# In the last quarter of a convolution, x comes doubled from DRAM instead of being doubled by VectorE

## The reference

```python
x = x + ffn(conv(x, cond_2048[:, None, :], b), w_router, w_experts)
# conv: depthwise causal convolution of 8 taps over the sequence, per channel, plus b
y = conv_general_dilated(x, w, window_strides=(1,), padding=[(K - 1, 0)], feature_group_count=D) + b
# ffn: each token goes to the one expert with the largest logit
idx = argmax(einsum('bsh,eh->bse', y, w_router))
out = take_along_axis(einsum('bsh,efh->bsef', y, w_experts), idx)
```

## Time and profile before

| | |
|---|---|
| median of three runs | 513.11 us |
| the profiled execution | 512.61 us, its span 510.8 us, mean granted clock 0.997 |
| TensorE busy | 502.5 us, 98% of the span |
| VectorE busy | 287.6 us (56%) |
| ScalarE busy | 150.5 us (29%) |
| GpSimd busy | 133.2 us (26%) |
| moved by DMA | 130.31 MB, mean 255 GB/s |

### The profile page before, as it was taken

How to read it: one execution, slowest core, us unless ns; L and a number is a source line. 1 busy time by engine, 2 the same in 40 slices (tenths; PEclk the granted TensorE clock), 3 DMA queues, 4 the chain that set the end, 5 groups by cost and what they waited for, 6 DMA issues and landing times.

```text
span 510.8 us, 9483 instructions
## 1 busy us (share of the span) xinstructions
PE 502.5 (98%) x2764; PEld 435.5 (85%) x2765; DVE 287.6 (56%) x418; ACT 150.5 (29%) x255; POOL 133.2 (26%) x148
## 2 busy tenths in 40 slices
PE   8999999999999999999999999999999999999995
PEld 8999999998888888888888888888888888888884
DVE  4947373769885233599753422863266343472961
ACT  2444444286101001365620000610043010340710
POOL 0004325063622111323311312203122322122222
PEclk9999999999999999999999999999999999999998
DMA  8977999999779999699998664695649655534445
GB/s 290 411 221 212 398 282 405 348 346 309 264 253 283 341 350 299 184 348 358 327 395 249 175 198 123 202 372 177 185 133 354 221 165 158 169 116 130 145 142 165
DMA packets 59623, 130.31 MB, mean 255 GB/s; under 512 B 12752, under 2 KB 32720, under 8 KB 59600
## 3 DMA queue, kind: packets, MB, share of 16 engines
q1 hardware_dynamic: 41696, 70.12, 44.3%
q0 software_dynamic: 14832, 54.27, 29.6%
q10 hardware_dynamic: 3072, 5.65, 3.5%
HBM read 94.56 MB, written 35.45 MB: 255 GB/s over the span
## 4 chain that ended last, share of the span: by engine, by line
PE 93%; DMA 5%; issue 0%; POOL 0%; DVE 0%; DVEq 0%; ACT 0%; SPq 0%; POOLq 0%
PE ps L858 75%; PE ps L814 18%; DMA y_sorted<-rows,pos_i 3%; DMA xs<-x_t 2%; DMA xs<-x_both 1%; POOL out L937 0%; DVEq L167 0%; DVE xs L516 0%; PE ps L829 0%; SPq L307 0%; ACT rows L438 0%; ACT part L437 0%; PE ps L826 0%; POOLq L978 0%; DVE x_row L702 0%
## 5 line engine op out<-in xcount | busy, mean ns | idle before, releaser
L858 PE MATMUL ps<-w_sb,ys 128*128 128x512 f32 x1680 | 381.6, 389 | 0.4 <-ACT rows L438 0.4
L858 PEld LDWEIGHTS ps<-w_sb,ys 128*128 128x128 f32 x1680 | 315.2, 188 | 66.1 <-ACT rows L438 0.5
L689 DVE STREAM_TRANSPOSE y_cols<-y_blk 128x1024 f32<-128x1024 f32 x36 | 44.8, 1243 | 140.1 <-PE ps L858 131.6
L814 PE MATMUL ps<-mats,xs 128*128 128x128 f32 x1024 | 117.8, 278 | 1.4 <-DMA xs<-x_both 1.1
L814 PEld LDWEIGHTS ps<-mats,xs 128*128 128x128 f32 x1024 | 116.9, 195 | 1.9 <-DVE mats L508 1.4
L451 ACT CAST ys<-y_cols 128x1024 fp32r<-128x1024 f32 x36 | 37.9, 1052 | 269.4 <-DVE y_cols L689 269.4
L680 DVE TENSOR_TENSOR w_sb<-w_raw,w_sb 128x1024 fp32r<-128x1024 f32 x56 | 64.2, 1218 | 3.3 <-ACT w_sb L446 3.3
L937 POOL DMA_INDIRECT out<-x_row,idx x35 | 40.8, 1165 | 80.3 <-DVE x_row L704 76.4
L944 POOL COPY idx<-ids_all 128x1 int32 (+1 forms) x36 | 15.2, 421 | 173.5 <-DMA out<-x_row,idx 118.7
L446 ACT CAST w_sb<-w_raw 128x1024 fp32r<-128x1024 f32 x56 | 56.4, 1050 | 9.5 <-PE ps L858 8.6
L925 POOL DMA_INDIRECT y_sorted<-rows,pos_i x32 | 35.3, 1103 | 78.1 <-PE ps L814 74.9
(11 more groups left out here) (102 smaller groups left out, 47.7 us busy)
## 6 DMA issues: line engine op xcount, KB each, us to landing
w_raw<-experts SPq DMA_DIRECT2D x56, 512.0 KB, 9.5
y_blk<-y_sorted SPq DMA_DIRECT2D x152, 128.0 KB, 3.4
xs<-x_both SPq DMA_DIRECT2D x15, 512.0 KB, 9.8
xs<-x_t SPq DMA_DIRECT2D x28, 256.0 KB, 7.0
xs<-x_t ACTq DMA_DIRECT2D x20, 256.0 KB, 7.5
w_first<-experts SPq DMA_DIRECT2D x8, 512.0 KB, 9.7
ids_all<-y_sorted SPq DMA_DIRECT2D x38, 1.0 KB, 4.5
x_row<-x_rows,idx POOLq DMA_INDIRECT x36, 4.6
```

The costliest lines, as they stand in the source:

```text
L689: V.transpose(y_cols[k][:, :, :].rearrange("p m (t i) -> p t m i", t=4), y_blk[k][:, :, :, :]).then_inc(y_blocks, 1)
L814: mm = nc.tensor.matmul(to, xs[:, n % X_RING, s % PACK, :], mats[:, s, :].rearrange("p (u n) -> p u n", n=SIDE), start=(s == sets[0]), sto ...
L858: return nc.tensor.matmul(out_ps[k][:, f * HALF:(f + 1) * HALF], ys[k][:, a, c, :], w_sb[:, c, b, f * HALF:(f + 1) * HALF], start=(c == 0 ...
```

## The change

In the last quarter too (packs 48 to 63) x comes from `x_both`: transfers of 512 KB over all 128 partitions in place of 256 KB over 64. VectorE makes no copies there, and TensorE waits for the transfer itself. Everything else stays: the queues, the ring, the order of issue.

```diff
-DOUBLED = PACKS
+DOUBLED = [n for n in range(4 * PACKS) if n < PACKS or n >= 3 * PACKS]
+SINGLE = [n for n in range(4 * PACKS) if n not in DOUBLED]
...
-    both = np.ones((DOUBLED, 2, PHASES, CH, PACK, GROUP, STEPS), x.dtype)
-    for n in range(DOUBLED):
-        both[n, 1 - n % 2] = cur[n]
-        both[n, n % 2, :PHASES - 1, :, :, :, 1:] = cur[n, :PHASES - 1, :, :, :, :-1]
-        both[n, n % 2, :PHASES - 1, :, :, :, 0] = 0.0
-    return both.reshape(DOUBLED, P, PACK * P), single[DOUBLED:]
+    both = np.ones((len(DOUBLED), 2, PHASES, CH, PACK, GROUP, STEPS), x.dtype)
+    for k, n in enumerate(DOUBLED):
+        both[k, 1 - n % 2] = cur[n]
+        both[k, n % 2, :PHASES - 1, :, :, :, 1:] = cur[n, :PHASES - 1, :, :, :, :-1]
+        both[k, n % 2, :PHASES - 1, :, :, :, 0] = 0.0
+    return both.reshape(len(DOUBLED), P, PACK * P), single[SINGLE]
...
-            if n < DOUBLED:
-                queue.dma_start(xs[:, s, :, :].rearrange("p c t -> p (c t)"), x_both[n]).then_inc(x_in[s], 16)
+            if n in DOUBLED:
+                queue.dma_start(xs[:, s, :, :].rearrange("p c t -> p (c t)"), x_both[DOUBLED.index(n)]).then_inc(x_in[s], 16)
...
             def double(n):
+                if n in DOUBLED:
+                    return
                 s = n % X_RING
...
-                    elif g == 0:
-                        pe.wait_ge(mats_ready, n + 2)
+                    elif n in DOUBLED:
+                        pe.wait_ge(mats_ready, min(n, PACKS - 1) + 2)
                         pe.wait_ge(x_in[n % X_RING], (n // X_RING + 1) * 16)
                     else:
                         pe.wait_ge(doubled, n - PACKS + 1)
```

More of the change, by code:

```diff
@@ L297, in load_x @@
                 queue.wait_ge(conv_mm, pack_done(n - X_RING))
-            if n < DOUBLED:
-                queue.dma_start(xs[:, s, :, :].rearrange("p c t -> p (c t)"), x_both[n]).then_inc(x_in[s], 16)
+            if n in DOUBLED:
+                queue.dma_start(xs[:, s, :, :].rearrange("p c t -> p (c t)"), x_both[DOUBLED.index(n)]).then_inc(x_in[s], 16)
             else:
                 side = (1 - n % 2) * SIDE
-                queue.dma_start(xs[side:side + SIDE, s, :, :].rearrange("p c t -> p (c t)"), x_t[n - DOUBLED]).then_inc(x_in[s], 16)
+                queue.dma_start(xs[side:side + SIDE, s, :, :].rearrange("p c t -> p (c t)"), x_t[SINGLE.index(n)]).then_inc(x_in[s], 16)
         def load_factors(queue, k):
```

## The result

The changed kernel takes 521.81 us (median of 4 runs, 518.67 to 522.23) against 512.89 us for the kernel before (median of 4): ratio 1.0155, 95% interval 1.0117 to 1.0193, so 8.9 us or 1.5% slower. The forecast was slower, 517.3 us. The direction and the reason (no room for 4.2 MB more in the stretch of the scatter) held; the place where TensorE stops, and half of the size, did not.

A forecast was written before the change was run, and what follows sets the result against it. TensorE, with expert matmuls and convolution, was taken to bound the kernel; 512.61 us plus 4.7 us lost at pack 57 gave 517.3 us, with a range of 511.5 to 523 us.

The forecast's parts named there:

- What bounds it, and the room: TensorE holds 93% of the chain of waits; no 20 us stretch has room for 2.36 MB more beside the scatter.
- the bound of 6.2 us: Upper bound of the scatter's delay from 81 to 101 us, if all loads go first; 4.2 us was taken.
- A third for each queue: POOL's, SP's and ScalarE's queues each get a third of 405 GB/s, 135 GB/s, beside the scatter.
- The term for the scatter: The last scatter of the second quarter's rows lands at 105.2 us, 4.2 us later, bounds 0 and 6.2.
- The other packs have 11.4 to 12.3 us from issue to use: Last quarter's packs other than 57: loads land in some 10 us, so nothing was added.
- the bank: TensorE wants the ring's sixth bank, evicted by ScalarE, at 103.1 us; 2.8 us late, inside the 4.7 us lost.
- pack 57: ScalarE issues its load after the scatter, at 105.2 us; 9.7 us to land, 4.7 us lost on TensorE.
- the sign that I had set: In the last quarter, TensorE's first stall on an even pack of SP's queue would show that the loads pay.
- The clock: Slower TensorE clock after a 3 to 5 us stall could cost 1.6 us; not summed, kept for the upper end.
- The loads pay: Rival, 0.20: the scatter keeps its rate, loads wait; TensorE waits 3.6 us at pack 56, giving 516.2 us.
- The bytes cost nothing: Rival, 0.32: half-wide loads hold the engines as long as whole ones, so last-quarter doubling is free, 512.4 us.
- What goes: VectorE's sixteen copies in the last quarter, some 11 us; only pack 57's 0.69 us lies on the path.

## Why the prediction was right or wrong

**What bounds it, and the room.** Right. With the bytes of before the convolution ends as before, with the added ones and the copies left in the whole loss is there, and the ceiling that I took (419 GB/s) is the one met (412 over 20 us, 420 over 8). One reading was off: ten loads are issued before 101 us, not nine, since pack 58's goes out at 98.97 us; the bound of 6.2 us would be 6.9.

**A third for each queue.** Right from 88 to 96 us (34.5, 34.0, 34.0%); over the whole of 81 to 101 us it is 37.9, 36.8 and 27.2%. The term for the scatter was 4.2 us; it measured 3.25 (104.25 against 101.00), and ScalarE's wait 10.58 where I said about 11. The Trainium skill (DMA: Bandwidth & Descriptors, Queues, rings and completion order) states that each engine goes round the queues it has work for. The trace agrees with that from 88 to 96 us.

**The step that failed** is "The other packs have 11.4 to 12.3 us from issue to use ... for some 10 us of landing; I add nothing." I had applied the third to the scatter and not to SP's queue, on which more stands than x. By the forecast's own numbers SP's queue gets 135 GB/s times 20 us, 2.7 MB, and it measured 3.04; the change asks it for 2.95 + 1.3 MB. The load of pack 52 has 512 KB of weights of the same stretch ahead of it; landing took 14.94 us, not 9.7, and 18.49 us for pack 60. TensorE therefore stopped at pack 52, and the two deadlines that I had priced (the bank, pack 57) were pushed back with it and did not bind: no stop near 103 us for an eviction, and the experts at 133.6 in place of 128. Both are real: they decide with the odd packs alone, and they come back once the weight load is moved. The price of 9.7 us for the load of pack 57 was good, 9.97 with the odd packs alone. By the sign that I had set, a first stall on an even pack of SP's queue speaks for the rival; what the runs show is a mix, the equal shares of my forecast and the late queue of the rival. That 521.81 us lies inside the range is in part luck: its upper end was made of a scatter 6.2 us late and a landing of 12.5 us for pack 57, and the time came from elsewhere.

**The clock.** I left it out of the sum and kept 1.6 us for the upper end. It was the larger part of the miss: 3.5 us of longer busy time, against waits of 6.6 us where my sum had 4.7. Of the 3.5, 1.46 us lie behind each of two waits. The rest is about what the broken pieces cost: at the pace of the unbroken 208 records in 23.47 us, 16 records are 1.81 us and took 2.03, and 64 are 7.22 and took 7.55 even at full clock. One of the four runs of the changed kernel had a mean clock of 1.0 and a span of 516.9 us, 3.5 us under the profiled one with 0.990. That the clock is behind the slow records is read from rows, since the run with TensorE kept busy decided nothing: the records are slow where the granted clock is 0.57 to 0.62 (behind waits of 2.28, 2.45, 2.62, 3.04, 3.66, 3.70 and 3.83 us) and not behind the wait of 2.72 us, where it stayed at 1.00.

**The rivals.** *The loads pay* had the queue right and the pack wrong (56 for 52), because it let the scatter keep its bytes. *The bytes cost nothing* is refuted beside the scatter, where the first eight packs alone lost 1.2%. It holds after the scatter, where the last eight cost nothing, at a share that hardly rises (0.98 to 1.02) for 20% more bytes. One reason can be read there. From 101.5 to 103.5 us SP's queue has the engines to itself, with the loads of packs 56 and 58 and a weight load behind them. In the kernel before, where the loads of x are half-wide (64 of the 128 partitions), and then in the kernel with the last eight packs doubled it moves (packets, MB, GB/s; then its share of the engines):

```profile
DMA packets 170, 0.42 MB, mean 212 GB/s; under 512 B 57, under 2 KB 70, under 8 KB 170
q1 hardware_dynamic: 170, 0.42, 105.3%
...
DMA packets 245, 0.75 MB, mean 375 GB/s; under 512 B 52, under 2 KB 65, under 8 KB 245
q1 hardware_dynamic: 245, 0.75, 103.2%
```

With the half-wide loads the engines were held as long for little more than half of the bytes. The Trainium skill (SBUF — State Buffer, Door 1: The DMA port swizzle) has half-wide transfers run at half the rate. The trace comes near that where the loads are alone. Beside the scatter it does not: from 81 to 101 us ScalarE's queue, which carries x alone, has 18.0% of the engines for its 1.35 MB of half-wide loads, the changed kernel 27.2% for 2.21 MB, and the kernel with the same bytes over all partitions (in 2 KB pieces) this:

```profile
q10 hardware_dynamic: 688, 1.39, 19.0%
```

That is 13.3, 12.3 and 13.7% a MB, so there whole loads cost about as much a byte as half-wide ones.

**What goes**, the copies, I had at nothing on the path, and that is what the run with the copies left in shows.

## What to carry to other kernels

Before moving work from an engine to DMA, take the GB/s of the very stretch in which the transfers fall, against the most that any stretch of the kernel reaches; the busy share says 1.0 with and without room. Where there is no room, add up every queue on its own, in its order of issue, at an equal share of the engines, and compare each load's landing with its deadline. Then count the slow matmuls that can follow a stop of TensorE: here they added some 1.5 us behind each of seven stops of 2.28 to 3.83 us, and nothing behind one of 2.72 us.

## What the runs showed of the hardware that I had not expected

Three queues with work got 34.5, 34.0 and 34.0% of the engines over 8 us, so what stands ahead of a load on its own queue can count for more than its size: 512 KB took 11.5 us on ScalarE's queue (median of 81 to 101 us) and, with other work ahead, 14.94 to 21.3 us on SP's. Small pieces hold a queue longer than their bytes tell: behind 512 KB in 1 KB pieces, a 256 KB load took 14.11 us, where the median of such loads on SP's queue was 7.0 us in the kernel before. And half-wide loads alone on the engines moved 212 GB/s where whole ones moved 375, at a busy share of about 1.0 in both; beside two other busy queues, all partitions in place of half of them made no such difference.
